# The last two stages of an eight-stage forward pass: a buffer per expert, half groups in the closing norms, two-tile additions on GpSimd

## What is computed

```python
x = x + jnp.tanh(g_xattn[3]) * _L3_xattn_ref(_layernorm(x), ctx_2048, ...)   # 16 heads, 64 keys and a null key
x = x + jnp.tanh(g_ffn[3]) * _L3_ffn_ref(_layernorm(x), Wr, W1, W2)
# _L3_xattn_ref ends:  out = out @ Wout;  (out - mu) * rsqrt(var + EPS) * ln_scale + ln_bias
# _L3_ffn_ref: 8 experts, 256 places each, one expert per row
eidx = argmax(softmax(xf @ Wr));  rank = place of the row among its expert's rows
xe = xf[dispatch];  ye = relu(xe @ W1) @ W2;  y.at[dispatch].add(ye * p * valid)
```

## Time and profile before

| | us |
|---|---|
| median of 3 runs | 918.8 (918.76 to 919.06) |
| the profiled execution, its own time | 916.99 |
| its span, first to last instruction | 915.3 |
| busy PE / DVE / ACT / POOL | 752.5 / 619.3 / 411.0 / 381.4 |

### The profile page before, as it was taken

One profiled execution on the slowest core, in us unless ns is written; L12 is line 12 of the kernel. 1 busy time (PEld: TensorE's weight loads), 2 busy tenths in 40 slices (PEclk: granted clock), 3 DMA queues, 4 the chain that ended last, 5 costly groups with the idle time before them and its releaser, 6 DMA issues. The chain is left out here.

```text
span 915.3 us, 14692 instructions
## 1 busy us (share of the span) xinstructions
PE 752.5 (82%) x4955; PEld 512.3 (56%) x4955; DVE 619.3 (68%) x1740; ACT 411.0 (45%) x904; POOL 381.4 (42%) x546
## 2 busy tenths in 40 slices
PE   3576999945889898998899788989999979986473
PEld 1555888823444454544434675656864447775363
DVE  4765322237788877774599975898877878985321
ACT  2134444412676666776246065535550027884310
POOL 6154433157655654510388333221110125673363
PEclk9968999976899999999999899999999989997697
DMA  8704776610000000000000000000020060011320
GB/s 190 282 23 130 219 215 201 212 38 6 19 13 13 8 13 3 1 1 2 1 0 1 1 1 1 0 1 1 1 69 0 1 183 1 1 48 47 92 58 26
DMA packets 52635, 48.59 MB, mean 53 GB/s; under 512 B 6900, under 2 KB 47751, under 8 KB 52306
## 3 DMA queue, kind: packets, MB, share of 16 engines
q1 hardware_dynamic: 49010, 40.06, 14.5%
q0 software_dynamic: 3552, 7.61, 3.0%
HBM read 38.47 MB, written 9.37 MB: 52 GB/s over the span
## 5 line engine op out<-in xcount | busy, mean ns | idle before, releaser
L1743 DVE TENSOR_REDUCE scratch<-psum 128x2 f32<-128x512 f32 (+1 forms) x160 | 106.4, 684 | 37.9 <-PE psum L1450 21.1
L1661 ACT ACTIVATE scratch<-psum 128x512 f32<-128x512 f32 x160 | 94.4, 603 | 67.4 <-PE psum L1470 67.4
L242 POOL TENSOR_SCALAR veps<-moments 128x4 f32<-128x4 f32 (+1 forms) x52 | 10.8, 208 | 236.2 <-DVE moments L163 234.4
L323 ACT ACTIVATE XT<-psum 128x512 f32<-128x512 f32 (+1 forms) x40 | 22.1, 561 | 118.6 <-PE psum L308 118.5
L946 DVE SCALAR_TENSOR_TENSOR scratch<-psum,b_block_bias,scratch 128x256 f32<-128x256 f32 (+1 forms) x48 | 18.6, 429 | 70.8 <-ACT scratch L1108 67.0
L1018 POOL DMA_INDIRECT scratch<-pair_rows,b_gather_at x39 | 39.2, 1005 | 64.2 <-PE psum L1162 41.3
L2621 PE MATMUL psum<-late,scratch 128*128 128x512 f32 x128 | 55.3, 592 | 0.0
L1470 PE MATMUL psum<-scratch,arena 128*128 128x256 bf16 x256 | 49.9, 277 | 5.4 <-ACT scratch L1641 4.4
L308 PE MATMUL psum<-ident,XN 128*128 128x128 f32 x144 | 26.9, 315 | 30.9 <-DVE XN L174 25.7
L245 POOL TENSOR_TENSOR rstd<-veps,minus_half 128x4 f32<-128x4 f32 (+1 forms) x52 | 49.3, 948 | 6.7 <-POOL veps L242 0.2
L1450 PE MATMUL psum<-arena 128*128 128x512 bf16 x128 | 50.6, 401 | 0.7 <-DVE scratch L1743 0.6
(11 more groups left out here) (474 smaller groups left out, 2028.3 us busy)
## 6 DMA issues: line engine op xcount, KB each, us to landing
arena<-in_L_ffn_w SPq DMA_DIRECT2D x72, 128.0 KB, 3.1
arena<-in_L_ffn_wg SPq DMA_DIRECT2D x24, 256.0 KB, 3.3
wide<-in_L_xattn_Wkv SPq DMA_DIRECT2D x1, 2048.0 KB
wide<-in_L_ffn_W SPq DMA_DIRECT2D x1, 2048.0 KB, 8.6
late<-in_L_ffn_W SPq DMA_DIRECT2D x8, 256.0 KB, 6.1
pair_results<-scratch SPq DMA_DIRECT2D x15, 128.0 KB, 3.3
folded_values<-arena SPq DMA_DIRECT2D x3, 512.0 KB, 4.7
scratch<-folded_values SPq DMA_DIRECT2D x3, 512.0 KB, 4.6
```

Source lines behind the costliest of these rows:

```text
L1661: a.activation(out, bank[3 + e % 2][:, :], ACT.Exp).then_inc(s["exp"], 1)
L1743: v.tensor_reduce(out, bank[m % 3][:, :].rearrange("p (h t) -> p h t", t=n), AX.X, ALU.max, negate=True).then_inc(s["maxed"], 1)
```

## The change

Three things are done.

1. **Dispatch.** The gathered rows get eight buffers instead of four (`ROWS = 8`), so the gather no longer waits for `copied`; it still waits for `turned` of expert e - 4, since four semaphores are shared. Six experts are gathered ahead of the first scatter (`AHEAD = 6`).
2. **Closing tiles in half groups.** The order of the norms is now given in half groups (`NORMS_ORDER`). Post 3 and following 3 are worked on two tiles at a time: statistics of tiles 12 and 13 come before DVE's additions of group 2, POOL takes their 1/sqrt between those of following 1 and 2, DVE adds them, and so on. The last four tiles of the next layernorm are normalized by DVE (`normalize_tiles`), no longer by ACT, so their POOL offsets fall away. PE turns and ACT copies the last two tiles apart, in a bank of their own; the router's products move by one place.
3. **Additions.** POOL's `add_half` scales and adds two tiles behind its divisions of tiles 8, 9, 11 and 12, where `add_group` took four behind tiles 9 and 13; ACT's normalizing of tiles 4 to 7 moves from steps 11, 12 to 10, 11; the 1/sqrt of following 0 moves from behind tile 12 to behind tile 13.

`group(g)` is replaced by `halves(g, half)`, which counts the same semaphores in half groups; in the earlier stages the counts and the instructions stay as they were.

```diff
-    OWN_AT = {7: (0, 1), 8: (2, 3), 11: (4, 5), 12: (6, 7)}
+    OWN_AT = {7: (0, 1), 8: (2, 3), 10: (4, 5), 11: (6, 7)}
+    NORMS_ORDER = (0, 1, 2, 3, 6, 7, 10, 13), (4, 5, 8, 9, 11, 12, 14, 15)
...
-            elif j in (9, 13):
-                self.add_group(g, q - 2)
-            elif j == 12:
+            elif j - 1 in self.OWN_AT:
+                self.add_half(g, j - 1)
+            elif j == 13:
                 self.following_pool(g, 0)
...
+        following = self.next.norm
         self.following_pool(g, 1)
+        self.post.pool_half(g, NG - 1, 0)
         self.following_pool(g, NG - 2)
-        self.post.pool_group(g, NG - 1)
-        self.following_pool(g, NG - 1)
+        self.post.pool_half(g, NG - 1, 1)
+        following.pool_half(g, NG - 1, 0)
+        following.pool_half(g, NG - 1, 1)
+    def add_half(self, g, step):
+        c, s, first = self.c, self.s, self.OWN_AT[step][0]
+        rows, sums = c.XN[:, first:first + 2, :], c.X[:, first:first + 2, :]
+        g.wait_ge(s["out_copied"], step + 1)
+        c.pool_chain.link(g, g.tensor_tensor(rows, rows, bc(self.affine[:, 0:1, :], (P, 2, D)), ALU.mult))
+        added = g.tensor_tensor(sums, sums, rows, ALU.add)
+        if first % GROUP:
+            added.then_inc(s["added"], 1)
...   (NullStage.dve, behind the loop)
-        last = range(NT - 2, NT)
+        following, scale = self.next.norm, self.affine[:, 0, :]
+        first, last = range(NT - GROUP, NT - 2), range(NT - 2, NT)
+        half_added = own.step(self.post.add_tiles(v, NG - 1, first, scale, c.X, 0))
         self.post.tile_stats(v, last, s["out_copied"])
-        self.post.add_to(v, NG - 1, self.affine[:, 0, :], c.X, s["added"])
+        v.wait_ge(own.sem, half_added)
+        following.tile_stats(v, first)
+        self.post.add_tiles(v, NG - 1, last, scale, c.X).then_inc(s["added"], 1)
         v.wait_ge(s["added"], NG)
-        self.next.norm.tile_stats(v, range(NT - GROUP, NT))
+        following.tile_stats(v, last)
+        following.wait_normed(v, NT - GROUP)
+        following.normalize_tiles(v, first)
+        following.normalize_tiles(v, last)
...   (DispatchStage)
+    ROWS = 8
     RING = 4
-    AHEAD = 4
+    AHEAD = 6
+    LAST_BANK = 2
...
             if e >= self.RING:
                 g.wait_ge(s["turned"], e - self.RING + 1)
-                g.wait_ge(s["copied"], self.TILES * (e - self.RING + 1))
...
-                g.indirect_dma_start(self.rows[:, e % self.RING, i, :, :]...
+                g.indirect_dma_start(self.rows[:, e, i, :, :]...
...   (DispatchStage.act)
         turn.act_group(a, 0)
+        self.norm.normalize_act(a, range(NT - 8, NT - GROUP))
         turn.act_group(a, 1)
-        self.norm.normalize_act(a, range(NT - 8, NT - GROUP))
         turn.act_group(a, NG - 2)
-        self.norm.normalize_act(a, range(NT - GROUP, NT))
-        turn.act_group(a, NG - 1)
+        turn.act_halves(a, 2 * NG - 2, 1)
+        turn.act_halves(a, 2 * NG - 1, 1, self.LAST_BANK)
```

More of the change, by code:

```diff
@@ L142, in interleave, with halves @@
         other.groups_before = self.groups_before
-    def group(self, g):
-        return self.groups_before + (self.stride * g if self.order is None else self.order[g])
+    def halves(self, g, half=1):
+        at = 2 * self.stride * g + half if self.order is None else self.order[2 * g + half]
+        return 2 * self.groups_before + at + 1
     def stats(self, v, g, ready=None):
@@ L171, in normalize, with normalize_tiles @@
             tiles = tiles[2 * half:2 * half + 2]
-        v.wait_ge(c.rstd_done, 2 * self.group(g) + (half + 1 if self.by_half else 2))
+        v.wait_ge(c.rstd_done, self.halves(g, half if self.by_half else 1))
+        for j in tiles:
+            v.tensor_scalar(self.dst[:, j, :], self.src[:, j, :], c.moments[:, j, 0:1],
+                            c.rstd[:, j:j + 1], ALU.subtract, ALU.mult).then_inc(c.normed, 1)
+    def normalize_tiles(self, v, tiles):
+        c, g = self.c, tiles[-1] // GROUP
+        v.wait_ge(c.rstd_done, self.halves(g, tiles[-1] % GROUP // 2))
         for j in tiles:
@@ L179, in add_to, with add_tiles @@
         self.add_tiles(v, g, range(GROUP * g, GROUP * g + GROUP), scale, sums).then_inc(done, 1)
-    def add_tiles(self, v, g, tiles, scale, sums):
+    def add_tiles(self, v, g, tiles, scale, sums, half=1):
         c, own = self.c, self.c.dve_chain
-        v.wait_ge(c.rstd_done, 2 * (self.group(g) + 1))
+        v.wait_ge(c.rstd_done, self.halves(g, half))
         for j in tiles:
@@ L197, in scaled @@
         tiles = range(GROUP * g, GROUP * g + GROUP)
-        v.wait_ge(c.moments_done, GROUP * (self.group(g) + 1))
+        v.wait_ge(c.moments_done, 2 * self.halves(g))
         for j in tiles:
@@ L640, in pe_group, with pe_half @@
         for j in range(GROUP * g, GROUP * g + GROUP):
+            last = t.matmul(c.bank[0][:, j * E:(j + 1) * E], c.XT[:, j * P:(j + 1) * P], weights,
+                            start=True, stop=True)
+        return last
+    def pe_half(self, t, half, turn, weights):
+        c = self.c
+        turn.wait_halves(t, half + 1)
+        for j in range(2 * half, 2 * half + 2):
             last = t.matmul(c.bank[0][:, j * E:(j + 1) * E], c.XT[:, j * P:(j + 1) * P], weights,
@@ L3401, in pe @@
         router.pe_group(t, 0, turn, weights)
+        turn.pe_group(t, 2)
         router.pe_group(t, 1, turn, weights)
-        turn.pe_group(t, 2)
+        turn.pe_halves(t, 2 * NG - 2, 1)
         router.pe_group(t, 2, turn, weights)
-        turn.pe_group(t, 3)
-        router.pe_group(t, 3, turn, weights).then_inc(c.logits_done, 1)
+        turn.pe_halves(t, 2 * NG - 1, 1, self.LAST_BANK)
+        router.pe_half(t, 2 * NG - 2, turn, weights)
+        router.pe_half(t, 2 * NG - 1, turn, weights).then_inc(c.logits_done, 1)
         t.wait_ge(s["chosen"], 1)
@@ L3426, in turn @@
             for i in range(self.TILES):
-                last = t.transpose(c.bank[6 + e % 2][:, i * P:(i + 1) * P], self.rows[:, e % self.RING, i, 0, :], c.ident[:])
+                last = t.transpose(c.bank[6 + e % 2][:, i * P:(i + 1) * P], self.rows[:, e, i, 0, :], c.ident[:])
             last.then_inc(s["turned"], 1)
```

43 lines of the change are left out of this document (19 added, 24 removed).

## The result

The changed kernel's median is 904.43 us (900.7 to 907.88, four runs) against 918.93 us (918.76 to 920.47, four runs): a ratio of 0.983 with a 95% interval of 0.981 to 0.985. The profiled execution took 903.62 us, its span 901.9.

A forecast was written before the change was run, and what follows sets the result against it. It took POOL and PE waiting for each other in the experts, PE's pace in the loop and a single closing thread as limits; 1.1 + 4.0 + 9.6 = 14.7 us less gave 904.1 us, range 901.2 to 907.8.

The forecast's parts named there:

- Eight buffers and six ahead: Experts: gathering six ahead fills POOL's idle time before the first scatter and ends PE's gather waits; 9.6 us less.
- POOL is what is late next, 0.9 us behind PE: Experts' end: PE ends by 893.7, POOL starts expert 7's first scatter at 894.6; last issue at 895.9.
- the signs: Profile checks named beforehand, such as no POOL idle over 0.35 us after twelve gathers, or late waits if PE bounds.
- Half groups: Closing norms and router: 8.5 us for 12.5, 4.0 us less, with PE's products at half clock (1.87 and 1.88).
- The thread of norms: Closing: POOL, DVE additions, statistics and normalizing let PE turn the first half 3.6 us after the last moments.
- the rival of full clock: Closing: clock stays full to the router's end, 6.4 us for 8.5, time 902.0; chance 0.15.
- DVE and POOL are off the path: Closing: last normalizing done 4.8 us after the moments, before PE finishes group 2's products, so PE's order sets the path.
- Additions: Attention loop: two-tile additions let POOL's divisions start earlier, cutting PE's waits at tiles 10 and 14; 1.1 us less.
- POOL's pieces in DVE's way: Attention loop: DVE loses 0.7 us at each of four places with half additions; 2.8 us back, 906.9; chance 0.12.
- The experts' rival: Experts: landings grow, and PE waits for expert 7 or POOL for last results; 1 to 3 us back; chance 0.10.
- nothing of the experts' gain: Experts: waits for `turned` hold POOL at gather 5 and the first scatter slides; 913.7; chance 0.04.
- slower: Experts: POOL's issue slows when up to twelve gathers follow without pause; 920.8 at 1.85 us per DMA; chance 0.02.

The follow-up runs named there:

- eight ahead: The changed kernel with all eight experts gathered ahead of the first scatter instead of six; median 905.45 us, ratio 0.985.
- dispatch only: The kernel before with only eight buffers and six experts gathered ahead; median 911.97 us, ratio 0.990.
- the last group whole: The changed kernel, but PE turns the last four tiles in one piece, behind group 2's products; median 905.22 us, ratio 0.981.
- keeping PE busy: The changed kernel with 30 unused multiplications of the unit matrix in PE's waits between router and first gather; median 904.68 us, ratio 0.984.
- additions only: The kernel before with only the two-tile additions at their new places; median 920.45 us, ratio 0.999.
- eight buffers only: The kernel before with eight buffers and no wait for copied, still four experts gathered ahead; median 921.02 us, ratio 1.001.
- DVE normalizes, only: The kernel before, whole groups kept, with the next layernorm's last four tiles normalized by DVE instead of ACT; median 919.60 us, ratio 0.998.

## Why the prediction was right, step by step

The time came out as forecast (904.4 for 904.1), and so did the order of the three terms. That the two times agree to 0.3 us is luck. The terms were mis-sized with errors that partly cancel: 1.8 us too little in the closing, 0.3 too little in the loop, 1.1 too much in the experts. That leaves 1.0 us more gain than the 14.7 of the sum, and the profiled execution lost 2.3 us ahead of tile 7, where the sum has nothing. The four executions themselves spread over 7.2 us.

Two slips of arithmetic bear on nothing: the low end adds up to 901.5, not 901.2, and the chances of the faster cases to 0.97.

*Eight buffers and six ahead: right mechanism, failed step "POOL is what is late next, 0.9 us behind PE".* The issue interval (1.31), the landing (2.9) and PE's end held: PE's last product ended 885.21 + 3.73 - 850.27 = 38.7 us after the first gather, for 893.7 - 855.16 = 38.5 predicted. But I compared PE with POOL for expert 7 alone. Its two scatters stand behind expert 6's two, and these need expert 6's result, which PE makes just ahead of the last (885.21, both in one row). In after POOL's issue came at 888.34, 1.27 us after half of those 3.73 us. So two of the signs failed: idle times above 0.35 us stayed (0.52, 0.49 and 1.25), and the late ones are those that were named for PE as the bound. By the prediction's own figures, PE's second product of expert 6 ends at 893.7 - 1.95 = 891.75; with 1.27 for DVE and the hand-over and three more issues of 1.29, the last issue is at 896.9, not 895.9: 8.7 us and not 9.6. The trace of before held the warning, a wait of POOL ahead of expert 6's first scatter:

```profile
901.71 0.98 POOL L3263 DMA_INDIRECT out_x<-scratch,h_scatter_at  x1 [1.25 <-DVE scratch L3348]
```

The other part of the miss is the clock: expert 1's first product took 2.52 in after (1.2 GHz to about 861.5), 2.38 with eight ahead, 2.11 in dispatch only, 1.99 with the last group whole, as in before; the experts of these four took 41.94, 41.81, 41.54 and 41.33 in the same order. PE's start passes to the end almost one to one, as it must where PE is the bound; keeping PE busy confirmed it.

*Half groups: failed term, the two products "1.87" and "1.88" at half clock.* The thread of norms was right: from the moments to the first turn 835.68 - 832.15 = 3.53 us, for 3.6. PE's part took 3.15 instead of 4.9: group 2's products 0.93 from start to start instead of 1.87, the turns 0.28 each instead of 0.4 and 0.56, the last products 1.66 instead of 1.88, and nothing for hand-overs. That is the rival of full clock, which I gave 0.15; its 6.4 us for the closing became 6.68, since the clock fell inside the last products. My argument for half clock was one row of one execution, and in the same old order that row isn't stable: group 2's products took 1.87 or 1.88 in before, dispatch only and additions only, but 1.06 in eight buffers only and DVE normalizes, only, on the same instructions. With half groups all six traces had 2.4 GHz there. Why those six agree stays open: PE's products then stand closer together, but no run varied that alone. With full clock DVE became as late as PE (836.83 and 836.89), so "DVE and POOL are off the path" no longer held.

*Additions: right, a little too small.* 1.42 and 1.39 for 1.1, within the bounds. The limit was ACT, as said: its copies of tile 14 start at 823.74 in after without a wait, where they waited 0.69. What I hadn't counted is that ACT's normalizing ahead of them came 0.6 us sooner after tile 7's copy, not 0.39: PE's idle time at tile 10 is less than its price, for tile 10's copy came 5.32 us after tile 9's in before and 4.71 in after.

*The rivals.* POOL's pieces in DVE's way: the mechanism is there and its price is not. DVE's L3163 takes 0.17 alone, but 0.44 to 0.52 at three of the four places with half additions; the DVE row at one of these and one without, then POOL's row:

```profile
801.34 0.52 DVE L3163 TENSOR_TENSOR arena<-arena,scratch 128x16 f32<-128x16 f32 x1
...
806.14 0.17 DVE L3163 TENSOR_TENSOR arena<-arena,scratch 128x16 f32<-128x16 f32 x1
```

```profile
801.11 0.72 POOL L2996 TENSOR_TENSOR X<-X,XN 128x256 f32<-128x256 f32 x1
```

DVE's instruction ends at 801.86, 0.03 us after POOL's (801.83). So it lost 0.35 us here. This delays POOL's next division by as much, and PE doesn't wait for it: 0 of the 2.8 us. The Trainium skill, SBUF — State Buffer, "Who interferes with whom", has the rule that a VectorE instruction with two SBUF inputs and a GpSimd instruction that reads SBUF exclude each other. By that rule the trace agrees in the 0.35 us. The experts' rival was half right, a loss of 1.1 from late results, but no landing grew. No wait for `turned` showed, and twelve issues in a row kept their 1.30 us, so the rivals "nothing of the experts' gain" and "slower" have nothing behind them.

*Ahead of tile 7: a term at nothing.* The prediction has all that the change touches behind the middle of the last cross-attention. The instructions bear that out and the traces don't: the last section has 3 to 4.6 us that go with the dispatch in these traces, and why stays open.

## What to carry to other kernels

When a queue of transfers on one engine alternates between feeding and draining another, read where each engine waits for the other, and run the feeding ahead until neither does: four experts to five brought 6.1 us, five to six 2.4, six to eight nothing. Before calling an engine the new bound, follow the last *two* results to the end, not the last one, and look in the trace of before for a wait that the edit leaves in place. A duration at the lower clock in one profile need not come again on the same instructions: compare the same row in several traces before building a term on it.

## What the hardware showed that I had not expected

*Stretches of identical instructions differ by several us from trace to trace, and the granted clock differs with them.* The start of tile 7's copy lay between 792.76 and 799.43 us over the eleven traces, each of another kernel. Early on this looks like scatter. Two kernels of the same chip that differ in `AHEAD` alone, in windows with PEclk as the third number from the end, first eight buffers only (794.86):

```profile
0.00:100.00 100.00, 61.09 (x318) 49.25 (x319) 59.53 (x220) 29.00 (x67) 44.46 (x92) 0.86 0.53 158
```

and dispatch only (799.43):

```profile
0.00:100.00 100.00, 62.58 (x299) 49.90 (x300) 57.29 (x211) 27.74 (x63) 43.65 (x91) 0.81 0.51 152
```

The later trace had the lower clock, 0.81 for 0.86. But DVE normalizes, only, had 0.81 too and the second earliest start (793.69), so this window alone does not order the traces.

Further on the traces fall into two groups. The same sixteen products of an earlier stage, in the same two kernels, first eight buffers only:

```profile
447.56 1.92 PE L2750 MATMUL psum<-g_Wout,arena 128*16 128x128 f32 x16
```

then dispatch only, where the granted clock fell from 1.00 to 0.50 while they ran:

```profile
449.11 3.55 PE L2750 MATMUL psum<-g_Wout,arena 128*16 128x128 f32 x16
```

They took 1.92 us in all five kernels that gather four experts ahead and 3.37 to 3.59 in all six that gather more. From their start to that of tile 7's copy it is 345.69 to 347.33 us in the five and 350.24 to 350.32 in the six, 3 to 4.6 us longer on the same instructions. In after these products started 1.8 us earlier than before, and the later loss of 4.2 turned that into the 2.34 us of the first table. What the order of POOL's DMAs 400 us later has to do with it, or whether the six and five fell so by chance, no run shows: dispatch only's median fell by 8.5 of the 8.9 us that its experts gained, which leaves little room for such a loss in every execution. So a stretch between two events says more about an edit of 1 us than the median does, but it is blind to what happens outside of it.

*Behind the same wait of 1.08 us on PE the loop took 37.65 or 39.28 us.* At tile 14 of the old additions the clock fell behind that wait in two of five traces, and with it went another 1.64 us. In both of these kernels, and in none of the other three, DVE normalizes the last tiles; whether that is more than chance stays open.
